# A one-core kernel of eight batches: its opening laid out anew

## Chip, cores and metric

The kernel runs on one core of a Trainium2 chip. The metric is the device time of one execution in microseconds (us), the median of the runs.

## What is computed

The input x has 8 batches of 512 rows of 256 values; ctx has 8 batches of 1601 rows of 256. Four layers follow each other, each added to x with a gain tanh(g), each on a layer norm of x:

```python
x = x + tanh(g_xattn[0]) * A(norm(x), ctx)   # one head: softmax(q Wq Wk' ctx' / 16 + mask) ctx Wv'
x = x + tanh(g_ffn[0])   * B(norm(x))        # self-attention, 4 of 16 heads of 64, picked per batch by a router
x = x + tanh(g_xattn[1]) * C(norm(x), ctx)   # 16 heads of 16 over ctx, integer mask shared by all batches
x = x + tanh(g_ffn[1])   * D(norm(x))        # mixture of 8 experts, each row to one, hidden size 1024
```

The router of B takes the mean of the normed x over the rows, times Wr, a softmax, and the 4 largest of 16. Everything is float32. In C the kernel splits q and k into three bfloat16 parts each, whose products give the scores.

## The kernel before, in words

Every engine has an instruction list of its own, written out in Python; semaphores tie them together. A batch of C is a loop of NU = 208 steps: 4 groups of 4 heads, 13 blocks of 128 ctx rows. Step u makes one transposed score of 99 x 128 x 512 in bfloat16 (`scores_t`, L1599), ACT takes its exponential (L1108), and every fourth step has the weighted sums of four heads (`values_c`, L1616). Ahead of the group that is being worked on, the scores of the next one are made once more, untransposed, in 64 pieces (`scores_c`, L1568), only for the row maxima, which DVE reduces (`maxima`, L2176); the table PIECES says how many pieces a step has. In and between these steps the layers A and B of the next batch (`prepare`) and the first part of A of the batch after it (`start_next`) are worked off; a Plan gives the step of each of their parts: XA, XB, XC the transposes of the normed x (`turn_x`, L1186) for A, B and C, QG the product with gA (`project_qg`, L1193), S the 16 scores of A (`score_a`, L1214), T the 16 transposes of their exponentials (`turn_a`, L1230), PV the 26 weighted sums of A (`weigh_a`, L1242), OA A's output product, K and V the projections of C (L1271, L1441), RL the router (L1281), QB, KB, VB, SB, TB, PVB, OB layer B (L1296, L1307, L1319, L1338, L1353, L1361, L1372), QC the query projection of C (L1389), LA, LB, LC the layer norms.

Before the loop there is the opening, W_END = 226 steps: batch 0 by the Plan FIRST, the beginning of batch 1 by SECOND, and from step 186 on the 64 first score pieces of batch 0 (W_PIECE), two a step. In each step every engine does `prepare(0, w, FIRST)`, then `start_next(0, w, FIRST)`, then `start_next(1, w, SECOND)`. The order in a list is the order of execution: an engine that waits holds up all that stands behind.

The layer norm goes from engine to engine: DVE makes statistics (L1897, L1903) and the variance (L1905), POOL the root (L819), DVE the normalisation (L1910), TensorE the transposes, ACT the copies out of PSUM (L967). PSUM has eight banks: MB (two), F0, F1, F2, SB (two), VB. In A of batch 0 the scores take turns in MB, F0, F1, the transposes in F2 and SB[0]; in A of batch 1 the scores take turns in F0 and F1 and all transposes are in F2. DVE adds the mask to a score and takes its maximum (`add_mask`, L1924); ACT makes the exponential (`exp_a`, L971), copies each transpose (`evac_pa`, L979, L982) and makes the high part of K (`high_k`, L989) into one of two buffers kp; DVE takes the rest (L1986), POOL splits it (L825, L827), SP stores the three parts (L592) to dramK. The query of C is kept in tq and qp, which lie in the place of ctxN; SP stores it with 6 DMAs per half (L614).

SP issues the weights, the stores, the loads of K, Q and V, and the gathered weights of B (L581, L585, after the router). POOL issues x, ctx, ctxT and the masks of A, in the order of its list. In the opening it also runs one `partition_all_reduce` (L911), whose result tells whether the mask of C hides anything. TensorE reads this flag ahead of step 186 and takes one of two copies of all that follows:

```python
            for w in range(W_PIECE[0]):
                open_step(w)
            pe.wait_ge(v_mf, 1)
            masked = pe.value_load(mflag[0:1, 0:1], min_val=0, max_val=1)
            pe.wait_ge(ld["ones"], 32)
            with pe.If(masked != 0):
                attend(True)
            with pe.Else():
                attend(False)
```

Of batch 1's 26 weighted sums of A, 7 stand in the opening (steps 216 to 224); the other 19 stand in steps 0 to 23 of the loop over batch 0, after which come A's output product (step 29) and the rest of batch 1.

## Time and profile before

| | |
|---|---|
| median of 3 runs | 2822.28 us (2820.21 to 2825.11) |
| the profiled execution | 2816.4 us, its span 2814.6 us |
| busy share of the span | TensorE 94%, DVE 61%, ACT 51%, POOL 10% |
| mean granted clock of TensorE | 0.989 of full |

The span is the time from the first to the last instruction. The opening takes the first 259 us of it, the loop over the batches follows, and the experts of layer D close it. TensorE's matmuls are pipelined: a group's busy time can be longer than the distance of its starts, and a float32 product is recorded as two passes.

### The profile page before, as it was taken

To read this page: it belongs to the slowest core of one execution; us is meant where nothing else is said; L and a number is where in the kernel's file an instruction comes from. 1 tells how busy PE (TensorE), PEld (TensorE's weight loads), DVE (VectorE), ACT (ScalarE), POOL (GpSimd) and SP (SyncE) were. 2 spreads that over 40 slices of the span, in tenths; PEclk is the share of its full clock that TensorE was granted. 3 is DMA by queue.
4 is the path that set the end of the run, shared out by engine and by line. 5 is a ranking of instruction groups with operands and counts; after the bars stand their busy time and mean duration, and the time that the engine had idled before them with its cause. 6 is when DMAs were issued, how large, how long until landed. Compare 5 with 4: busy or idle time off the path is not lost.

```text
span 2814.6 us, 39400 instructions
## 1 busy us (share of the span) xinstructions
PE 2632.1 (94%) x13626; PEld 1283.8 (46%) x13626; DVE 1729.8 (61%) x4198; ACT 1447.7 (51%) x2923; POOL 281.8 (10%) x344
## 2 busy tenths in 40 slices
PE   7878999999999999999999999999999989999998
PEld 3534433344334434443335433443444323349998
DVE  3346677577765776667666776677666768853111
ACT  2232565546554565456554656456545745663332
POOL 1200100011000200020001100020002000002221
PEclk9988999999999999999999999999999999999999
DMA  5431322423132413241232313241224023169995
GB/s 185 119 102 53 88 58 56 109 61 98 42 110 53 120 41 99 55 122 34 79 92 64 88 42 110 60 120 42 90 57 104 19 52 74 34 205 375 369 363 169
DMA packets 215140, 296.36 MB, mean 105 GB/s; under 512 B 50533, under 2 KB 180813, under 8 KB 214934
## 3 DMA queue, kind: packets, MB, share of 16 engines
q1 hardware_dynamic: 198428, 221.50, 28.1%
q0 software_dynamic: 16512, 72.32, 7.5%
q8 instruction: 110, 1.80, 0.3%
q14 instruction: 90, 0.74, 0.1%
HBM read 232.87 MB, written 60.50 MB: 104 GB/s over the span
## 4 chain that ended last, share of the span: by engine, by line
PE 78%; DVE 9%; ACT 6%; issue 5%; SPq 1%; DMA 1%; POOL 0%; ACTq 0%; POOLq 0%; DVEq 0%
PE PS L1616 12%; PE PS L1568 10%; PE PS L1599 10%; PE PS L1242 7%; DVE mxC L2176 6%; PE PS L1214 6%; PE PS L1751 5%; PE PS L1761 5%; PE PS L1271 3%; PE PS L1441 2%; PE PS L1338 2%; PE PS L1361 2%; ACT reg L1108 2%; PE PS L1230 2%; ACT reg L995 2%
## 5 line engine op out<-in xcount | busy, mean ns | idle before, releaser
L1108 ACT ACTIVATE reg<-PS 128x512 f32<-128x512 f32 (+1 forms) x1664 | 962.3, 598 | 946.2 <-PE PS L1599 940.0
L2176 DVE TENSOR_REDUCE mxC<-PS 128x1 f32<-128x400 f32 (+1 forms) x2048 | 1091.0, 570 | 529.4 <-PE PS L1568 513.6
L1568 PE MATMUL PS<-reg 96*128 96x400 bf16 (+1 forms) x2048 | 665.3, 339 | 51.6 <-DVE mxC L2176 20.8
L1599 PE MATMUL PS<-reg 99*128 99x512 bf16 (+1 forms) x1664 | 606.7, 384 | 23.0 <-ACT reg L1108 18.5
L1616 PE MATMUL PS<-reg 128*17 128x512 f32 (+1 forms) x3328 | 439.6, 600 | 1.1 <-DVE reg L2200 0.7
L1568 PEld LDWEIGHTS PS<-reg 96*128 96x128 bf16 x2048 | 195.2, 98 | 519.9 <-DVE mxC L2176 375.5
L1599 PEld LDWEIGHTS PS<-reg 99*128 99x128 bf16 (+1 forms) x1664 | 164.0, 100 | 351.0 <-ACT reg L1108 191.1
L1214 PE MATMUL PS<-reg 128*128 128x512 f32 (+1 forms) x512 | 209.8, 524 | 14.5 <-DVE small L1924 13.8
L1242 PE MATMUL PS<-reg 128*128 128x512 f32 (+1 forms) x416 | 211.5, 601 | 0.7 <-ACT reg L982 0.7
L1141 ACT ACTIVATE reg<-PS,reg 128x128 f32<-128x128 f32 x312 | 89.0, 368 | 197.9 <-PE PS L1751 110.4
L1751 PEld LDWEIGHTS PS<-reg 128*128 128x128 f32 x1248 | 145.0, 192 | 2.7 <-issue 0.9
L1751 PE MATMUL PS<-reg 128*128 128x128 f32 x1248 | 146.0, 275 | 0.0
L1761 PE MATMUL PS<-reg 128*128 128x256 f32 x624 | 141.6, 378 | 0.0
L1214 PEld LDWEIGHTS PS<-reg 128*128 128x128 f32 x512 | 88.8, 193 | 80.8 <-issue 51.1
L1761 PEld LDWEIGHTS PS<-reg 128*128 128x128 f32 x624 | 115.2, 189 | 15.0
L1616 PEld LDWEIGHTS PS<-reg 128*17 128x17 f32 (+1 forms) x3328 | 55.2, 95 | 145.3 <-issue 107.9
L819 POOL TENSOR_TENSOR rstd<-vpe,mhalf 128x4 f32<-128x4 f32 x32 | 33.1, 1034 | 857.6 <-DVE vpe L1905 847.9
L1924 DVE CUSTOM_DVE_ANT_0 reg<-PS,reg 128x512 f32<-128x512 f32 (+1 forms) x128 | 72.6, 570 | 72.1 <-PE PS L1214 69.4
L1271 PE MATMUL PS<-reg,wkC 128*128 128x400 f32 (+1 forms) x256 | 103.1, 513 | 6.0 <-DVE reg L1986 6.0
L1992 DVE TENSOR_REDUCE nmB<-PS 128x1 f32<-128x512 f32 x128 | 84.8, 682 | 26.3 <-PE PS L1338 26.3
L1441 PE MATMUL PS<-wvC,reg 128*128 128x256 f32 (+1 forms) x416 | 100.1, 379 | 0.0
L1242 PEld LDWEIGHTS PS<-reg 128*128 128x128 f32 (+1 forms) x416 | 76.1, 193 | 49.9 <-issue 40.0
(268 smaller groups left out, 2513.9 us busy)
## 6 DMA issues: line engine op xcount, KB each, us to landing
reg<-in_D_W SPq DMA_DIRECT2D x78, 1024.0 KB
reg<-in_A_mask POOLq DMA_DIRECT2D x32, 800.5 KB, 6.6
dramK<-reg SPq DMA_DIRECT2D x144, 100.0 KB
dramV<-reg SPq DMA_DIRECT2D x48, 272.0 KB, 3.1
reg<-in_ctxT POOLq DMA_DIRECT2D x8, 1601.0 KB, 9.7
reg<-in_ctx POOLq DMA_DIRECT2D x8, 1536.0 KB, 7.7
dramQ<-reg SPq DMA_DIRECT2D x96, 128.0 KB
reg<-dramQ SPq DMA_DIRECT2D x32, 384.0 KB, 5.8
```

The source lines that it names most:

```text
L1108: act.activation(pr[u % RING][0:r, :], PS[0:r, S_PLAN[NU * b + u][0], :], ACT.Exp).then_inc(a_expC, 1)
L1141: act.activation(hT[:, m, :], PS[:, bank, at:at + TS], ACT.Relu, bias=b1[par][:, m:m + 1]).then_inc(a_h, 1)
L1214: last = mm(PS[:, ring_a(n, i), 0:w], qgA[:, k, t * P:(t + 1) * P], ctxT[:, k, c0:c0 + w], start=k == 0, stop=k == KD - 1)
L1242: last = mm(PS[:, FB[m], :], ctxN[0:r, c, m * P:(m + 1) * P], ptA[0:r, c, :], start=c == 0, stop=c == CT - 1)
L1271: last = mm(PS[:, k_bank(n, u), 0:w], wkC[:, k, m * P:(m + 1) * P], ctxT[:, k, c0:c0 + w], start=k == 0, stop=k == KD - 1)
L1441: last = mm(PS[0:rows(c), v_bank(n, i), c % 2 * D:(c % 2 + 1) * D], ctxT[:, k, c * P:c * P + rows(c)], wvC[:, k, :], start=k == 0, stop=k ...
L1568: last = mm(PS[:, bank, 0:w], qs[(NG * bb + g) % 3][0:ROWS, h, t * P:(t + 1) * P], ks[g % 2][0:ROWS, h, c0:c0 + w], start=True, stop=True)
L1599: last = mm(PS[0:r, bank, :], ks[g % 2][0:STK, h, c * P:c * P + r], qs[(NG * b + g) % 3][0:STK, h, :], start=True, stop=not with_mask)
L1616: last = mm(PS[32 * h:32 * h + DC + 1, VB, :], vc[0:r, c, g * GH + h, :], pr[(UN * g + GH * c + h) % RING][0:r, :], start=c == 0, stop=c = ...
L1751: last = mm(PS[:, bank, at:at + TS], w1[j % WB][:, k, m * P:(m + 1) * P], xsT[j % 2][:, k, :], start=k == 0, stop=k == KD - 1)
L1761: last = mm(PS[:, VB, 0:D], hT[:, m, :], w2[j % WB][:, m, :], start=m == 0, stop=m == FM - 1)
L2176: v.tensor_reduce(mxC[:, h, t, j:j + 1], PS[:, M_PLAN[bb, g, i][0], 0:M_CH[j][1]], AX.X, ALU.max).then_inc(v_mx, 1)
```

## The change

- x of batch 0 is the first DMA of SP (it was one of POOL's), and DVE scales gA at step 7, behind the layer norm, and no longer first.
- Transposes of A take turns in three banks, in batch 0 (F2 and both SB) and in batch 1 (F2, VB, F0). Batch 1's scores have VB and SB[1] for the first two and then MB and SB. The two halves of the normed x of batch 0 are transposed into two banks, F2 and F1. ACT's exponential of a tile stands one step before that tile's first transpose.
- The K parts of batch 0 have eight buffers, in places of memory that are not yet in use; two K projections stand after the first four V projections. The sum for the router comes from ACT's copies (accum_out), not from a reduction on DVE.
- tq and qp of batch 0 lie elsewhere, so that ctxN of batch 1 loads from step 77, behind batch 0's weighted sums. Half of batch 0's Q stores are issued by ACT.
- Batch 1's masks each have a buffer: two are loaded by POOL at step 48, two by SP at step 147.
- qg and the first scores of batch 1 stand in layer B of batch 0 (steps 139 to 148); the branch stands ahead of step 152, in the layer norm of C, and no longer ahead of 186.
- The first score pieces of batch 0 go to steps 194 to 225. All 26 weighted sums of batch 1 stand in the opening: 18 in steps 206 to 224, four ahead of the transposes of the row maxima (step 231) and four behind. The opening has 237 steps.

The diff, cut:

```diff
-FIRST = Plan(SC=49, OA=(75, 77), LB=79, XB=(86, 88), RL=92, K=[78, 80, 94, 96, 98, 99, 100, 101],
-             V=[79, 81, 82, 90, 93, 95, 97], QB=(104, 105), KB=(106, 107), VB=(108, 109), LA=0, XA=(7, 9),
+FIRST = Plan(SC=49, OA=(75, 77), LB=79, XB=(86, 88), RL=92, K=[85, 87, 94, 96, 98, 99, 100, 101],
+             V=[78, 79, 81, 82, 90, 95, 97], QB=(104, 105), KB=(106, 107), VB=(108, 109), LA=0, XA=(7, 9),
              SB=O_SB, TB=[O_SB[i // 2] + 6 + 2 * (i % 2) for i in range(16)], PVB=(O_SB[3] + 11, O_SB[7] + 11),
              OB=(150, 151), LC=153, QG=(10, 12), XC=(161, 163), QC=(165, 167),
              S=[14, 15, 16, 17, 18, 19, 20, 21, 26, 27, 28, 29, 34, 35, 36, 37],
              T=[22, 23, 24, 25, 30, 31, 32, 33, 38, 39, 40, 41, 43, 44, 45, 46],
              PV=[48 + c for c in range(2 * CT)], wrap=0, ctx=0)
-SECOND = FIRST._replace(LA=100, XA=(112, 115), QG=(153, 155),
-                        S=[168, 170, 172, 174] + [178 + 10 * t + d for t in range(3) for d in (0, 2, 4, 6)],
-                        T=[178 + 10 * t + 2 * j for t in range(QT) for j in range(4)],
-                        PV=[216 + c for c in range(sum(u < NU for u in U_PV))], ctx=180)
+SECOND = FIRST._replace(LA=100, XA=(112, 115), QG=(139, 142),
+                        S=[145, 148, 164, 166] + [170 + 8 * t + d for t in range(3) for d in range(4)],
+                        T=[174 + 8 * t + d for t in range(3) for d in range(4)] + [198, 200, 202, 204],
+                        PV=[206 + c * 20 // 18 for c in range(18)] + [226, 227, 228, 229] + [232, 233, 234, 235], ctx=77)
 U_RAMP, U_MARK, U_RANK, U_SUM, U_TAB, U_SLOT = 2, 41, 46, (60, 75, 90, 112, 126, 140), (156, 157), (158, 159, 160, 161)
 U_TJ, U_ONE, U_IDS, U_WL = (162, 163, 164, 165, 166), (167, 168, 169, 170, 171, 172, 173), 190, (157, 158, 159)
-W_PIECE, W_ROWS = (186, 218), 222
-W_END = 226
+W_BRANCH, W_PIECE, W_ROWS = 152, (194, 226), 231
+W_END = 237
...
         return (MB + (F0, F1))[i % 4]
-    return (F0, F1)[i % 2] if n == 1 else F0
+    if n == 1:
+        return (VB, SB[1])[i] if i < 2 else (MB + SB)[(i - 2) % 4]
+    return F0
 
 
 def turn_a_bank(n, i):
 
     if n == 0:
-        return (F2, SB[0])[i % 2]
-    return F2 if n == 1 else F1
+        return ((F2,) + SB)[i % 3]
+    return (F2, VB, F0)[i % 3] if n == 1 else F1
+
+
+def qg_bank(n, k):
+
+    return (VB, SB[1])[k] if n == 1 else (F0, F1)[k]
+
+
+def x_bank(L, k):
+
+    return (F2, F1)[k] if L in (norm_a(0), norm_b(0), norm_c(0)) else F2
...
+                return eA0[t]
+            return eA0[(t + 2) % 4] if n == 1 else eA[t % 2]
...
+        kp0 = kp + [regC[:, w0:w0 + KPW].bitcast(BF16).rearrange("p (r c) -> p r c", r=3)
+                    for w0 in [k_at + KPW * i for i in range(5)] + [q_at]]
+        qg1 = regC[:, kr_at:kr_at + KD * S].rearrange("p (k q) -> p k q", k=KD)
...
+            sp.dma_start(xin, a["x"][0:1].rearrange("o (t p) n -> p (o t) n", p=P)).then_inc(ld["x0"], 16)
             sp.dma_start(qgA, a["A_WqWk"].rearrange(k2, p=P)).then_inc(ld["a"], 16)
...
-                    sp.wait_ge(kd_stored[i], 48 * (4 * n + 2 * (g // 2) + half + 1))
+                    sp.wait_ge(kd_stored[i], 48 * (4 * n + 2 * (g // 2) + half + 1 if n else 4))
...
+                    if n or r < NR // 2:
+                        sp.dma_start(dramQ[n, 8 * m:8 * m + 8, r * DC:(r + 1) * DC, :],
+                                     q_part(n, m, part)).then_inc(qd_stored[m], 16)
...
+                if w == SECOND.PVB[1] + 1:
+                    sp.wait_ge(pe_pvB, 2)
+                    for t in (2, 3):
+                        sp.dma_start(wA(1, t), a["A_mask"][1, t * P:(t + 1) * P, :]).then_inc(ld[f"mq{t}"], 16)
...
-            load_x(0)
             load_ctxT(0)
...
+                if m == 1 and u == 48:
+                    pool.wait_ge(pe_ptA, 16)
+                    load_mask(m, 0)
+                    load_mask(m, 1)
+                if m > 1 and u == p.PVB[1] + 1:
...
+                if m == 1 and u == p.ctx:
+                    pool.wait_ge(pe_otA, 2)
+                    load_ctx(m)
+                if m > 1 and u == p.ctx:
...
+            def evac_sum(L, k):
+                act.wait_ge(pe_xT, 2 * L + k + 1)
+                act.activation(xT[:, k, :], PS[:, x_bank(L, k), :], ACT.Copy,
+                               accum_out=msum[:, k:k + 1]).then_inc(a_xT, 1)
...
-                past(act, kd_stored[u % 2], 48 * (4 * n + u // 2))
-                act.activation(kp[u % 2][:, 0, 0:w], PS[:, k_bank(n, u), 0:w], ACT.Identity,
+                if n:
+                    act.wait_ge(kd_stored[u % 2], 48 * (4 * n + u // 2))
+                elif u == 2:
...
-                    if u + p.wrap == p.PV[CT * (k + 1) - 1] + 1:
-                        act.wait_ge(pe_otA, 2 * n + k + 1)
-                        act.activation(otA[:, k, :], PS[:, (F0, F1)[k], :], ACT.Copy).then_inc(a_otA, 1)
+                    if n != 1 and u + p.wrap == p.PV[CT * (k + 1) - 1] + 1:
+                        evac_ota(n, k)
...
-                    if u == p.S[4 * t + 3] + 2:
+                    if u == (p.T[4 * t] - 1 if m < 2 else p.S[4 * t + 3] + 2):
...
+                for m in range(KD):
+                    if w == FIRST.QC[m] + 6:
+                        act.wait_ge(v_qs, m + 1)
+                        for r in range(NR // 2, NR):
+                            act.dma_start(dramQ[0, 8 * m:8 * m + 8, r * DC:(r + 1) * DC, :],
+                                          q_part(0, m, QPART[r])).then_inc(qd_stored[m], 16)
...
-                elif n == 1:
-                    pe.wait_ge(v_ttr, 16 * n + i - 1)
-                elif n == 0:
-                    past(pe, v_ttr, i - 3)
-                if n == 1 and i < 2:
-                    pe.wait_ge(v_tq, i + 1)
-                elif n > 1 and i:
+                elif n == 0 and i >= 4 or i >= 5 and n == 1:
+                    pe.wait_ge(v_ttr, 16 * n + i - 3)
...
-                    past(pe, a_ptA, 16 * n + i if n else i - 1)
+                    past(pe, a_ptA, 16 * n + i - (2 if n < 2 else 0))
...
-                if p.wrap and u + p.wrap in p.PV:
+                if n > 1 and u + p.wrap in p.PV:
...
-                for w in range(W_PIECE[0], W_END):
+                for w in range(W_BRANCH, W_END):
...
-            for w in range(W_PIECE[0]):
+            for w in range(W_BRANCH):
...
-                if u == p.XB[1] + 2:
-                    dve.wait_ge(a_xT, 2 * norm_b(n) + 2)
-                    v.tensor_reduce(msum, xT, AX.X, ALU.add).then_inc(v_ms, 1)
...
-            dve.wait_ge(pe_set, KD)
-            v.tensor_scalar(gA[:], PS[:, 0:KD, 0:D], 1.0 / 16.0, None, ALU.mult).then_inc(v_set, 1)
+            def scale_g():
+                dve.wait_ge(pe_set, KD)
+                v.tensor_scalar(gA[:], PS[:, 0:KD, 0:D], 1.0 / 16.0, None, ALU.mult).then_inc(v_set, 1)
...
+                if w == 7:
+                    scale_g()
```

## Rows read from the trace of the kernel before

**Rows 1.** The page: busy time of the engines, and TensorE's slices.

```profile
PE 2632.1 (94%) x13626; PEld 1283.8 (46%) x13626; DVE 1729.8 (61%) x4198; ACT 1447.7 (51%) x2923; POOL 281.8 (10%) x344
...
PE   7878999999999999999999999999999989999998
```

**Rows 2.** Busy time of each engine in two stretches (start:end, length, engines, clock, DMA).

```profile
core 0: us, PE busy (x) PEld busy (x) DVE busy (x) ACT busy (x) POOL busy (x), PEclk, DMA share, GB/s
0.00:258.80 258.80, 205.24 (x716) 109.24 (x716) 118.00 (x296) 71.34 (x137) 32.46 (x49) 0.93 0.37 117
258.80:296.00 37.20, 36.33 (x141) 13.49 (x142) 20.00 (x39) 14.61 (x25) 0.00 (x0) 0.95 0.21 53
```

**Rows 3.** Timeline from 0 to 40 (start, length, engine, line; idle before and its cause).

```profile
9.17 1.39 DVE L1897 BATCH_NORM_STATS2 st<-reg 128x6 f32<-128x256 f32 x4
...
17.59 5.26 PE L1193 MATMUL PS<-reg,gA 128*128 128x512 f32 x8 [0.69 <-ACT reg L967]
...
23.54 11.41 PE L1214 MATMUL PS<-reg 128*128 128x512 f32 x32 [0.69 <-ACT reg L1009]
```

**Rows 4.** DMA issues from 0 to 60: KB each, us to landing.

```profile
reg<-in_A_WqWk SPq DMA_DIRECT2D x1, 512.0 KB, 3.9
reg<-in_x POOLq DMA_DIRECT2D x1, 512.0 KB, 7.2
```

**Rows 5.** TensorE's timeline from 34 to 63, batch 0's transposes.

```profile
34.79 1.04 PE L1230 MATMUL PS<-ident,reg 128*128 128x128 f32 x8
...
38.17 0.33 PE L1230 MATMUL PS<-ident,reg 128*65 128x128 f32 x1 [1.44 <-ACT reg L979]
...
47.43 7.41 PE L1214 MATMUL PS<-reg 128*128 128x512 f32 x16
...
62.58 22.63 PE L1242 MATMUL PS<-reg 128*128 128x512 f32 x52 [0.69 <-ACT reg L982]
```

**Rows 6.** Timelines of TensorE, ACT and SP around the K projections.

```profile
117.75 5.61 PE L1271 MATMUL PS<-reg,wkC 128*128 128x400 f32 x8 [6.01 <-DVE reg L1986]
...
116.34 0.59 ACT L989 ACTIVATE reg<-PS,bkC 128x400 bf16<-128x400 f32 x1 [6.87 <-DMA dramK<-reg]
...
108.78 2.53 SPq L585 DMA_DIRECT2D bs<-in_B_b  x4
```

**Rows 7.** TensorE's timeline from 165 to 187, around normalisation C.

```profile
165.07 3.72 PE L1372 MATMUL PS<-woB,reg 128*128 128x256 f32 x16 [0.85 <-DVE reg L2117]
...
178.04 1.09 PE L1186 MATMUL PS<-ident,reg 128*128 128x128 f32 x4 [5.81 <-issue]
...
186.66 6.07 PE L1214 MATMUL PS<-reg 128*128 128x512 f32 x16
```

**Rows 8.** Timelines of DVE and POOL there.

```profile
171.67 0.17 DVE L1905 TENSOR_SCALAR vpe<-mv 128x4 f32<-128x4 f32 x1
...
138.09 0.38 POOL L911 PARTITION_ALL_REDUCE small<-small  x1 [8.38 <-issue]
...
175.47 1.05 POOL L819 TENSOR_TENSOR rstd<-vpe,mhalf 128x4 f32<-128x4 f32 x1 [9.65 <-issue]
```

**Rows 9.** Timelines of TensorE and DVE, from 201 to 260.

```profile
205.88 1.49 PE L1568 MATMUL PS<-reg 96*128 96x400 bf16 x4 [4.69 <-issue]
...
258.82 0.39 PE L1599 MATMUL PS<-reg 99*128 99x512 bf16 x1 [2.94 <-DMA reg<-mrow]
...
215.58 0.69 DVE L1924 CUSTOM_DVE_ANT_0 reg<-PS,reg 128x512 f32<-128x512 f32 x1 [2.52 <-DMA reg<-in_A_mask]
...
244.45 7.85 DVE L2176 TENSOR_REDUCE mxC<-PS 128x1 f32<-128x400 f32 x16 [0.17 <-PE PS L1568]
```

**Rows 10.** Groups of instructions from 258.8 to 296 (count, busy us, mean ns, idle before).

```profile
L1242 PE MATMUL PS<-reg 128*128 128x512 f32 (+1 forms) x38 | 21.0, 634 | 0.0
L2176 DVE TENSOR_REDUCE mxC<-PS 128x1 f32<-128x400 f32 (+1 forms) x37 | 19.8, 570 | 21.1 <-PE PS L1568 21.1
```

**Rows 11.** Stretches of 5 us with a low clock (columns as in rows 2).

```profile
225.00:230.00 5.00, 5.00 (x14) 2.68 (x15) 2.47 (x6) 1.29 (x3) 0.00 (x0) 0.66 0.02 9
...
240.00:245.00 5.00, 4.73 (x18) 2.98 (x18) 4.42 (x10) 1.91 (x4) 0.00 (x0) 0.50 0.00 0
```

99 lines of the change are left out of this document (68 added, 31 removed).

## The prediction

> **What bounds the kernel now.** I read the page first: TensorE is busy for 94% of the span, and the slices show that it has room in two places only, the first four of the forty and two near the end [rows 1]. The change touches nothing near the end, so the question is what the opening costs. I cut it into two stretches [rows 2]: up to batch 0's first transposed score (258.8 us; TensorE is busy for 205.2, part of that at the lower of its two clock levels, 1.2 instead of 2.4 GHz), and the next 37.2 us, in which 19 weighted sums of batch 1 stand (busy 36.3). An instruction taken out of the loop is worth its full length if TensorE sets the pace there; put into a hole of the opening it costs nothing. Then I went along TensorE's timeline and asked at each hole which engine ended it [rows 3 to 9].
>
> **Start.** DVE begins x's statistics at 9.17, behind the scaling of gA, which waits for the setup products. x itself took 7.2 us from its issue on POOL, against 3.9 for A_WqWk, first on SP [rows 3, 4]. With x first on SP I let it land at 4.7, as A_WqWk did, and A_WqWk, now behind it and beside ctxT, at 7.0 to 8.0. The normalised x is there near 9.5, but the setup products (3.8 us) stand ahead of the transposes on TensorE and end at about 11.2. The transposes take 2.2, with a bank each and so without the copy between them, then copy 0.7, qg 3.4 to 5.3 (3.4 at 2.4 GHz; 5.26 before, half of it at 1.2 [rows 3]) and copy 0.7: first score at 18.2 instead of 23.54. **−5.3** (−3.5 to −6.5).
>
> **Batch 0's transposes.** One tile's four transposes are 1.6 us of work, but from 34.79 to the next score there are 3.6: ACT has the next tile's exponential between two copies, and TensorE waits up to 1.44 for a bank [rows 5]. With three banks, and the exponential issued behind the fourth copy, beside the next scores, the wait goes at two tiles: −3.9. The 16 products at 47.43 took 7.41 against half of 11.41 for 32 at 23.54 [rows 3, 5], since the clock fell behind such waits: −1.7. At the last two tiles the exponential follows the copies and is waited for in one piece: 6.9 instead of 7.9, from 54.67 to 62.58. **−6.5** (−3 to −8).
>
> **K and V projections.** TensorE waits 6.01 before 117.75 because ACT waited 6.87 for a store of K out of one of two kp buffers, and the next 8 products run cold, 5.61 instead of 2.8 [rows 6]. Eight buffers remove both, 8.8. A second bank for the transposes of x and ACT's sum in place of DVE's reduction remove 1.0 (a wait for a copy as the 0.69 before qg [rows 3], and a short one for the sum); the sum adds 0.2 to two copies, under a V projection of 1.7. Next late are the gathered weights: SP issues the four loads of biases behind those of the weights, until 111.3 [rows 6], and by my count the last lands 11.5 behind the routing product, whose end moves with TensorE, while K7 is through 10.8 behind it. That gives back 0.7 (0 to 3). If POOL's two operations per K fall behind, the range takes it in. **−9.1** (−6 to −10).
>
> **Batch 0's FFN attention.** It gains two qg products and two scores of batch 1, 4 × 1.74 = 6.9 of work on TensorE (a pass of 512 columns takes 22.63 / 52 = 0.435 [rows 5], each has four), among waits for copies and divisions of 0.5 to 0.85, of which the last is [rows 7], 3.1 together. **+3.9** (+3 to +6; ACT has two more copies in a full stretch).
>
> **Normalisation C.** From the end of the output projection (168.8) to the transposes at 178.04 are 9.25 us, though DVE has the variance at 171.84. POOL's root starts at 175.47 with "issue" as its cause, 9.65 after the mask DMAs; the same POOL lost 8.38 before its all-reduce at 138.09 [rows 7, 8]. I read this as POOL changing its program to the all-reduce and back, the way back starting only once the queue is past mask loads that wait for batch 0's second weighted sum. The change takes these loads away from here (two to step 48, two to SP); the way back starts behind the all-reduce and is over some 25 us before the root, which then follows the variance: 3.0 and the 2.6 from root to transposes, 5.6 instead of 9.25. **−3.6** (0 if the way back waits for the variance). The branch cost TensorE 4.69 where it stood [rows 9]; it lies in these 5.6 now, which hold no other work of TensorE, and is covered with 0.9 to spare. Without that cover it costs up to 4.69. The Q projections then take 9.4 from their first transpose, against 8.6 to 186.66 [rows 7]: two scores of batch 1 more (1.9), two waits for copies less. **+0.8** (−1 to +3, by how long the clock stays low).
>
> **From the Q projections to the first transposed score.** Before: 186.66 to 258.82, 72.2 us: the branch, products at half clock behind it, DVE held for batch 1's third mask until 215.58, so that the maxima run only from then on, and 2.94 for the copy of the row maxima [rows 9]. That mask's load stood behind POOL's wait for both Q stores. After: masks and ctxN are there. Twelve scores and transposes of batch 1, three times 5.6 + 1.6 [rows 3, 5], 21.8. Then 64 first scores in 32 steps: 12 steps by DVE (24 maxima × 0.49, from 16 in 7.85 [rows 9]), 11.8; 20 steps by TensorE (40 × 0.17 and 18 weighted sums × 0.87), 22.5. Four more sums 3.5, transposes 0.3, and four sums (3.5) that cover the 2.94. Sum 63.3. **−8.9** (−2 to −13). The six Q store issues on ACT stand before its copies while TensorE has scores for 5.6: nothing, and by SP's pace (0.6 each [rows 6]) 3.8 if uncovered.
>
> Opening: −5.3 − 6.5 − 9.1 + 3.9 − 3.6 + 0.8 − 8.9 = −28.7; first transposed score at 230.
>
> **Loop.** 38 passes × 0.435 = 16.5 leave its first 37.2 us [rows 10]. Its 37 maxima take 18 to 20 of DVE, the exponentials 14.6 of ACT [rows 2, 10], and TensorE keeps some 17 of work. Step by step, with the slowest of the three (ACT 2.4 for steps 0 to 3; DVE 4.0, 4.5, 4.5 for the next twelve; TensorE 2.7 and 2.7), it becomes 20.9: **−16.4** (−9 to −17). Later steps keep their work.
>
> Sum −45.1. The clock also fell to the low level at 225 and at 240, in the stretch that DVE paces [rows 11]; more such holes stand in the new one and in the loop's first steps: +3 (0 to 8). For waits that the trace of before can't show (code fetched behind a moved branch, DMA issues on ACT, banks shared by the two batches): +2 (0 to 6). −40.1: the profiled execution goes from 2816.4 (span 2814.6) to 2776; it stands 5.9 under the median of the runs, 2822.3, so I predict 2782.
>
> **Rivals.**
> (a) *The loop gives little back.* First and transposed scores wait for each other in turn through the two MB banks, DVE at 0.6 to 0.7 a maximum; the 24 steps take 29 and 8 is lost: 2790. Against: TensorE idles for only 0.9 of the 37.2 [rows 2].
> (b) *The next late thing in the opening.* POOL's way back still in the norm (3.6), weights late by 3, crowding in the attention (2): +8.6, 2791.
> (c) *Slower: TensorE's clock.* If waits short and often held it at 1.2 GHz from the Q projections to the loop's step 24, its work there (22 + 30 + 7 + 17) would double, less 11 that lie under DVE's pace: +65, 2847; the sign turns when the low level lasts for some 45 us of that work. For it: 0.50 at 240, 0.66 at 225 [rows 11]. Against: it was back within 5 us each time. The Trainium skill ("TensorE: Matmul & The Clock Gate", on oscillation) has a kernel with short pieces of work between waits fall to the low clock at every piece; by that rule this rival is the outcome, and the trace bears it out in part only.
> (d) *More*: no unseen waits and the clock high throughout: 2771.
>
> The Trainium skill ("Runtime: NRT & Kernel Launch", instruction fetch mechanics) says that a taken branch breaks the sequential fetch and stalls for a load of code; the 4.69 of the trace agree.
>
> **Numbers.** Forecast 0.54 (its own range 2774 to 2790), (a) 0.14, (b) 0.16, (c) 0.03, (d) 0.11, a gain under 0.2% 0.02. Two measurements of this kernel tell apart about 0.2%, 5.6 us. Range 2768 to 2800. Faster 0.95, same 0.02, slower 0.03.
>
> **What would show it.** In the profile after: first score near 18; no wait of 1.4 among the transposes of batch 0's first two tiles; K projections without a hole and at most a small one for the gathered weights before QB; POOL's root right behind the variance; an "issue" hole of about 5.6 before norm C's transposes and none before the first scores; no DVE wait for a mask; first transposed score near 230 and the loop's first 24 steps in some 21. It is wrong if those stay over 28, or if the first scores and sums (36 to 40 us) take over 48.

## The result and the profile of the changed kernel

| | before | after |
|---|---|---|
| median | 2821.24 us (4 runs, 2815.25 to 2825.11) | 2778.44 us (4 runs, 2776.35 to 2781.13) |
| the profiled execution | 2816.4 us, span 2814.6 | 2776.35 us, span 2774.5 |

The ratio is 0.9851, with an interval of 0.9831 to 0.987: 43 us less. 2782 was forecast. The two spans differ by 40.1 us, and a ledger of them can be made by the starts of the same instructions on TensorE in both traces. The last column is what the prediction had for the part.

| part, from and to which start on TensorE | before | after | difference | forecast |
|---|---|---|---|---|
| 0 to the first score of batch 0 | 23.5 | 16.8 | −6.7 | −5.3 |
| to its first weighted sum | 39.0 | 32.1 | −6.9 | −6.5 |
| weighted sums, to the first K or V projection | 26.9 | 26.9 | 0 | 0 |
| K and V projections, to the gathered product (QB) | 33.7 | 26.2 | −7.6 | −9.1 |
| batch 0's FFN attention, to its output projection | 41.9 | 46.3 | +4.4 | +3.9 |
| output projection and normalisation C, to its transposes | 13.0 | 11.0 | −2.0 | −3.6 |
| Q projections | 8.6 | 7.9 | −0.7 | +0.8 |
| to the first transposed score | 72.2 | 64.1 | −8.0 | −8.9 |
| loop, to batch 1's output product of A | 42.1 | 29.9 | −12.2 | −16.4 |
| the rest | 2513.7 | 2513.3 | −0.4 | 0 |
| clock and waits that could not be seen | | | in the rows above | +5 |

Each row rests on one execution of each kernel, and some rows are less sharp than they look. A second trace of the changed kernel has a span of 2774.2 us, but 27.6 us for the K and V projections (26.2 here) and 40.2 us from the first score piece to the first transposed score (41.8 here). The trace of the first experiment below, whose code is that of the kernel before in the first two parts, has 25.2 and 37.3 us there instead of 23.5 and 39.0: the sum is the same, the split between the two is not.

The page's busy row and slices, to be read beside [rows 1]: TensorE does the same 13626 instructions, and the first slices are fuller.

```profile
PE 2617.1 (94%) x13626; PEld 1276.9 (46%) x13626; DVE 1721.6 (62%) x4190; ACT 1447.8 (52%) x2939; POOL 280.3 (10%) x341
...
PE   8989999999999999999999999999999989999998
```

The two stretches of [rows 2], with the columns told there, cut at the first transposed score (231.3) and here at batch 1's output product (261.2):

```profile
0.00:231.30 231.30, 204.80 (x754) 110.67 (x755) 119.28 (x295) 69.96 (x140) 30.32 (x46) 0.98 0.43 132
231.30:261.20 29.90, 25.72 (x123) 6.15 (x122) 22.32 (x45) 17.16 (x31) 0.00 (x0) 1.00 0.30 73
```

The opening now holds 38 passes more (754 instead of 716) and is 27.5 us shorter. TensorE's busy time in it is the same, because the clock is 0.98 in place of 0.93. In the second stretch TensorE was busy for nearly the whole time before; now 4.2 of 29.9 us are holes.

The timelines answer to [rows 3], [rows 5] and [rows 9]. x's statistics begin at 4.84 instead of 9.17; qg's products take 3.71 and not 5.26; the transposes of the first tile (28.04) stand in one piece with the third tile's scores right behind; the first score piece of batch 0 (189.50) has no stall in front of it.

```profile
4.84 1.41 DVE L1976 BATCH_NORM_STATS2 st<-reg 128x6 f32<-128x256 f32 x4 [3.26 <-DMA reg<-in_x]
...
12.41 3.71 PE L1271 MATMUL PS<-reg,gA 128*128 128x512 f32 x8 [0.69 <-ACT reg L1018]
...
28.04 1.62 PE L1306 MATMUL PS<-ident,reg 128*128 128x128 f32 x13
29.50 5.71 PE L1288 MATMUL PS<-reg 128*128 128x512 f32 x16
...
189.50 0.85 PE L1647 MATMUL PS<-reg 96*128 96x400 bf16 x4
```

Around the K projections ([rows 6] before), TensorE, ACT and SP. The hole of 6.01 is gone, but one of 1.85 stands in its place. ACT waits 3.09 for a store of V, and SP issues that store at 93.19, behind six issues for K that took 3.83.

```profile
98.95 2.93 PE L1349 MATMUL PS<-reg,wkC 128*128 128x400 f32 x8 [1.85 <-DVE reg L2067]
...
97.28 0.38 ACT L1087 ACTIVATE reg<-PS 65x256 f32<-65x256 f32 x1 [3.09 <-DMA dramV<-reg]
...
89.32 3.83 SPq L632 DMA_DIRECT2D dramK<-reg  x6
93.19 0.46 SPq L661 DMA_DIRECT2D dramV<-reg  x1
...
98.06 2.53 SPq L625 DMA_DIRECT2D bs<-in_B_b  x4
```

Around normalisation C ([rows 7, 8] before): POOL's root starts at 155.04, right behind DVE's variance (154.77, which takes 0.17), where it came 3.6 us late before. But POOL's next operation, the residual with its bias (L886), runs from 156.08, and DVE's normalisation beside it takes 3.07 where it takes 1.38 without (8.25, in the start).

```profile
159.30 1.94 PE L1259 MATMUL PS<-ident,reg 128*128 128x128 f32 x8 [7.40 <-DVE reg L1989]
...
154.77 0.17 DVE L1984 TENSOR_SCALAR vpe<-mv 128x4 f32<-128x4 f32 x1
156.13 3.07 DVE L1989 TENSOR_SCALAR reg<-reg,mv,rstd 128x256 f32<-128x256 f32 x4 [1.19 <-POOL rstd L863]
...
8.25 1.38 DVE L1989 TENSOR_SCALAR reg<-reg,mv,rstd 128x256 f32<-128x256 f32 x4 [1.30 <-POOL rstd L863]
...
L1989 DVE TENSOR_SCALAR reg<-reg,mv,rstd x4: 404/404/2097, 156.1 to 158.8; 128x256 f32<-128x256 f32 x4
...
155.04 1.06 POOL L863 TENSOR_TENSOR rstd<-vpe,mhalf 128x4 f32<-128x4 f32 x1 [39.10 <-DVE vpe L1984]
156.08 2.00 POOL L886 TENSOR_TENSOR reg<-reg,boC 128x1024 f32<-128x1024 f32 x1
```

The line without a start gives the shortest, median and longest of DVE's four in ns: one took 2.10 us, the others 0.40 each, as in the start. In the kernel before, the same addition of POOL came 45 us behind the normalisation, since the loads of ctxN and of two masks, with their waits, stood ahead of it in POOL's list:

```profile
221.84 2.01 POOL L842 TENSOR_TENSOR reg<-reg,boC 128x1024 f32<-128x1024 f32 x1
```

The change took those loads away from there, and so brought the addition beside the normalisation.

Behind the Q projections, the Q stores that ACT now issues hold its exponential for 3.04, and TensorE waits 1.07 for it:

```profile
173.99 1.67 PE L1306 MATMUL PS<-ident,reg 128*128 128x128 f32 x13 [1.07 <-ACT reg L1027]
...
169.14 3.02 ACTq L1187 DMA_DIRECT2D dramQ<-reg  x3
172.21 1.63 ACT L1027 ACTIVATE reg<-reg,small 128x1601 f32<-128x1601 f32 x1 [3.04 <-issue]
```

In the loop's first steps DVE's maxima come in runs with holes of 0.68 between them, and each hole lies beside a set of weighted sums on TensorE (L1695, 1.05):

```profile
238.12 4.63 DVE L2256 TENSOR_REDUCE mxC<-PS 128x1 f32<-128x400 f32 x9 [0.68 <-PE PS L1647]
243.43 1.59 DVE L2256 TENSOR_REDUCE mxC<-PS 128x1 f32<-128x400 f32 x3 [0.69 <-PE PS L1647]
...
242.07 1.05 PE L1695 MATMUL PS<-reg 128*17 128x512 f32 x8
```

### The profile page after: what moved, and what is told of

Its sections match the earlier page's. It is cut to its first block, busy times and chain, and to the rows that moved or that the text cites. A ratio compares the mean times of both kernels' runs of the same rounds, so it can differ in the third digit from the quotient of the medians.

```text
span 2774.5 us, 39396 instructions
## 1 busy us (share of the span) xinstructions
PE 2617.1 (94%) x13626; PEld 1276.9 (46%) x13626; DVE 1721.6 (62%) x4190; ACT 1447.8 (52%) x2939; POOL 280.3 (10%) x341
## 4 chain that ended last, share of the span: by engine, by line
PE 78%; DVE 9%; ACT 6%; issue 4%; SPq 2%; DMA 1%; POOL 0%; ACTq 0%; POOLq 0%; DVEq 0%
PE PS L1695 12%; PE PS L1647 10%; PE PS L1678 10%; DVE mxC L2256 7%; PE PS L1320 7%; PE PS L1288 6%; PE PS L1830 5%; PE PS L1840 5%; PE PS L1518 2%; PE PS L1415 2%; PE PS L1349 2%; PE PS L1438 2%; ACT reg L1175 2%; PE PS L1306 2%; PE PS L1430 2%
## 5 line engine op out<-in xcount | busy, mean ns | idle before, releaser
L1695 PE MATMUL PS<-reg 128*17 128x512 f32 (+1 forms) x3328 | 439.5, 600 | 1.1 <-DVE reg L2280 0.7
L1288 PE MATMUL PS<-reg 128*128 128x512 f32 (+1 forms) x512 | 204.4, 515 | 14.3 <-DVE small L2005 13.4
L1320 PE MATMUL PS<-reg 128*128 128x512 f32 (+1 forms) x416 | 211.1, 600 | 0.8 <-ACT reg L1038 0.8
L1695 PEld LDWEIGHTS PS<-reg 128*17 128x17 f32 (+1 forms) x3328 | 55.2, 95 | 144.5 <-issue 107.7
```

The costliest lines, as they stand in the source:

```text
L1288: last = mm(PS[:, ring_a(n, i), 0:w], qg(n)[:, k, t * P:(t + 1) * P], ctxT[:, k, c0:c0 + w], start=k == 0, stop=k == KD - 1)
L1320: last = mm(PS[:, FB[m], :], ctxN[0:r, c, m * P:(m + 1) * P], ptA[0:r, c, :], start=c == 0, stop=c == CT - 1)
L1695: last = mm(PS[32 * h:32 * h + DC + 1, VB, :], vc[0:r, c, g * GH + h, :], pr[(UN * g + GH * c + h) % RING][0:r, :], start=c == 0, stop=c = ...
```

## The experiments

The spans of single executions can be told apart only so far. In the unchanged loop, the distance between the output products of A of two batches is 302.8 us for most pairs (300.3 to 300.9 for the first), but 0.3 to 2.9 more for one to three pairs of each trace, and the last 700 us (697.1 to 700.4) differ by up to 3.3 us between traces. So an edit is judged by its own part of the ledger, and by whole times only where several runs stand behind them. Even a part can differ between traces with the same code in it, by 2 us and more at the K and V projections; where that matters, the other traces are named.

### POOL's way back to its ordinary program

To the kernel before, one small addition on POOL right behind the all-reduce, so that the ordinary program is wanted there and not only at the root:

```diff
 pool.partition_all_reduce(..., bass.bass_isa.ReduceOp.max).then_inc(g_set, 1)
+pool.tensor_tensor(small[:, 40:44], mhalf[:], mhalf[:], ALU.add).then_inc(g_set, 1)
```

> The kernel before, with one tiny POOL addition (128x4) right behind the all-reduce, so that POOL meets an ordinary instruction there and not first in normalisation C. Theory (POOL changes its program to the all-reduce and back, and the way back starts only when an ordinary instruction comes up in the queue): the addition carries a hole of 8 to 10 us, and the root of normalisation C starts within 0.2 us of the variance instead of 3.6 behind it; the stretch from the end of the output projection to the transposes goes from 9.25 to 5.6 us, 3.6 less in the total. Rival (the two mask loads keep POOL busy writing descriptors for 9.6 us): the root stays 9.6 us behind the mask issues, the stretch stays 9.2.

Measured: 2815.87 us, 2819.69 for the kernel before beside it, one run each, within the spread of the kernel before (2815.25 to 2825.11). POOL's timeline (compare [rows 8]):

```profile
137.64 0.38 POOL L911 PARTITION_ALL_REDUCE small<-small  x1 [7.63 <-issue]
145.94 0.19 POOL L913 TENSOR_TENSOR small<-mhalf 128x4 f32<-128x4 f32 x1 [7.92 <-issue]
...
172.00 1.06 POOL L819 TENSOR_TENSOR rstd<-vpe,mhalf 128x4 f32<-128x4 f32 x1 [6.11 <-DVE vpe L1906]
```

The addition takes the 7.92 us upon itself, the root stands right behind the variance, and the transposes of C start at 174.58, 3.5 sooner. The loss behind the all-reduce is the cause of the late root, and not the mask loads, which stand where they stood. It comes with the next ordinary instruction, not when the all-reduce ends. In the changed kernel that instruction is the root itself, which waits 39.10 for the variance, and the loss is hidden in this wait. That it is a change of POOL's program is a reading of these rows; they show the loss, not what it is made of. The root is forward here too, and no addition of POOL meets the normalisation (it comes at 220.44): TensorE's transposes start 9.4 behind its output projection, against 11.0 in the changed kernel. The mask behind which DVE waited came 3.9 sooner as well (211.65 and 215.58), yet the first transposed score comes only 0.4 sooner. The windows say where the rest went: the same 127 passes from the mask to that score.

```profile
211.60:258.40 46.80, 38.80 (x127) 19.20 (x127) 33.84 (x81) 9.04 (x15) 2.55 (x2) 0.78 0.06 19
```

and in the kernel before:

```profile
215.50:258.80 43.30, 34.83 (x127) 17.58 (x127) 33.80 (x81) 9.03 (x15) 2.54 (x2) 0.88 0.07 21
```

TensorE's granted clock was 0.78 here and 0.88 there, and its passes took 4.0 us longer in sum, which is as much as the 3.5 that went missing.

The start of this trace says one thing more. Its code there is that of the kernel before, with the same holes among the transposes, yet the fourth tile's 16 products, which took 7.41 there [rows 5], are these:

```profile
49.11 5.71 PE L1215 MATMUL PS<-reg 128*128 128x512 f32 x16
```

In their place qg's products took 6.77 and not 5.26. The fall of the clock that the kernel before had at these products belongs to that execution, not to its holes.

### The residual copy held back

To the changed kernel:

```diff
 pool.wait_ge(v_oB, QT * (b + 1))
+if b == 0:
+    pool.wait_ge(v_xn, 4 * norm_c(0) + 4)
```

> The kernel after, with POOL's addition of the bias to the residual of batch 0 (128x1024, 2.0 us) held until DVE has normalised for layer C. In the kernel after it starts 1 us ahead of that normalisation's end and DVE's four instructions take 3.07 us instead of 1.38. Theory (the two engines slow each other when they read and write the same memory at once): the four take 1.4, the hole before TensorE's transposes goes from 7.4 to 5.7. Rival (DVE is slow there for another reason, such as the code that is loaded for TensorE's branch at the same time): they stay near 3.1.

Measured: 2775.82 us. DVE's normalisation and POOL's copy:

```profile
154.93 1.38 DVE L1991 TENSOR_SCALAR reg<-reg,mv,rstd 128x256 f32<-128x256 f32 x4 [1.19 <-POOL rstd L863]
...
156.83 2.00 POOL L888 TENSOR_TENSOR reg<-reg,boC 128x1024 f32<-128x1024 f32 x1 [1.94 <-DVE reg L1991]
...
156.41 1.94 PE L1261 MATMUL PS<-ident,reg 128*128 128x128 f32 x8 [5.71 <-DVE reg L1991]
```

The normalisation is back at 1.38, and TensorE's hole is 5.71 instead of 7.40, which is the 5.6 that the prediction had. So the collision alone cost the 1.7. The first transposed score came 2.4 sooner, and the loop to batch 1's output product took 31.9 instead of 29.9 in this execution (a clock of 0.71 and 0.61 from 230 to 240).

### A third bank in the loop's first steps

To the changed kernel: F2, free by then, as a third bank for the maxima of batch 0's first 40 steps, beside the two MB, with the two waits of TensorE that the bank then needs.

```diff
-window = spare_at(u)
+window = 3 if b == 0 and u < 40 else spare_at(u)
```

> The kernel after, with F2 as a third bank for the untransposed scores of batch 0's first 40 steps. In the kernel after, DVE idles 0.7 us behind each set of four weighted sums (1.0 us of TensorE), nine maxima take 5.3 instead of 4.5 us, and the first 24 steps take 25 us instead of the 20.9 forecast. Theory (two banks are too few to carry DVE over the sums): the idle goes at most sets, the first 24 steps take 21 to 22.5 and the first product behind them (A's output, at 261.2) starts 3 us sooner. Rival (DVE's own pace of 0.5 to 0.57 per maximum is the bound): 24 to 25, nothing moves.

Measured: 2773.75 us. DVE:

```profile
236.90 4.42 DVE L2260 TENSOR_REDUCE mxC<-PS 128x1 f32<-128x400 f32 x9 [0.25 <-PE PS L1651]
```

The hole in each run falls from 0.68 to 0.25, a maximum from 0.51 to 0.49, and the part from 29.9 to 26.7: −3.2. Of the 4.2 us that the loop gave back too little, the two banks hold at least three quarters.

### SyncE's order at the K and V projections

Two edits of one line, alone and in the changed kernel: the stores of batch 0's first two K pieces behind step 96 (behind V's store and the gathered weights), or behind step 92 (behind V's store only).

```diff
-if u == p.K[i] + 3:
+if u == (96 if n == 0 and i < 2 else p.K[i] + 3):
```

> The kernel after, with SP's stores of the first two K pieces put behind the loads of the gathered weights. In the kernel after, TensorE has a hole of 1.85 us before the last two K projections: ACT's copies of K stand behind its copy of V, which waits for a V store that SP issued late, behind six K store issues (3.8 us). The gathered weights come late by the same 3.8. Theory (both come from SP's order): the hole closes, layer B's first projection starts 1.5 to 2.0 us sooner. Rival (the hole is the store's own landing time, 4 us among other transfers): hole and start stay within 0.5.

Measured: 2776.71 us. The last K product set stands without a hole and the weights are issued from 92.21 on (94.95 in the changed kernel); V/K to QB takes 23.8 instead of 26.2. The 26.2 is one trace. In six others with the changed kernel's code there, the part takes 24.9, 25.2, 25.2, 25.6, 25.8 and 27.6, with a hole of 1.37 to 1.95 ahead of the last K products each time; with the stores moved it takes 23.8 here and 23.9 in the last experiment's kernel of four edits. Against these seven traces the edit is worth 1.1 to 3.8 us, mostly between 1 and 2.4.

> The changed kernel with the stores of the first two K pieces of batch 0 put behind step 92 of SyncE's order, so that the store of the fourth piece of V is issued ahead of them and not behind their six issues. All K stores but these keep their places. The theory (TensorE's hole of 1.85 us in the K and V part comes by way of ScalarE's V copy, which waits for a V store that SyncE issues late) expects that hole gone and the part to last about 24 us from the first K or V product to the router's gathered product, as where the two stores went to step 96 (23.8 instead of 26.2), and the ends of the batch 0 part 2 us sooner. The rival (the gathered weights, issued last, are what the part waits for) expects a hole of about 1 to 2 us just ahead of the gathered product, since the six issues now stand between V's store and the weights again. Span 2771 to 2775, since spells of low clock further on differ by up to 3 us between executions.

Measured: 2776.71 us. With step 92, TensorE and SP:

```profile
93.66 5.89 PE L1349 MATMUL PS<-reg,wkC 128*128 128x400 f32 x16
101.59 0.70 PE L1373 MATMUL PS<-reg 128*128 128x512 f32 x1 [2.04 <-DMA bs<-in_B_b]
...
89.19 3.83 SPq L632 DMA_DIRECT2D dramK<-reg  x6
94.58 2.91 SPq L621 DMA_DIRECT2D reg<-in_B_w  x4
97.67 2.53 SPq L625 DMA_DIRECT2D bs<-in_B_b  x4
```

V's store went ahead, all 16 K products run in one piece, and the 1.85 are gone. But now the gathered weights end TensorE's wait, 2.04: the part takes 25.8, the rival's reading. Both waits come from the same six issues on SP. Only with them behind both the store and the weights is the time saved. They are not enough by themselves, though: in the trace of the two transposing banks below, SP's order is the changed kernel's, V's store is issued 15.7 us behind the part's first product instead of 17.4 and lands 3.4 behind that instead of 4.1 (ACT waits 1.29 for it and not 3.09), all 16 K products run in one piece, and the part takes 24.1. What makes the store earlier there stays open. The gain of the first of the two edits did not reach the end in its only execution: 3.6 us ahead at the first transposed score (1.6 of it in score pieces that the edit does not touch), 2.2 at batch 1's output product (clock 0.82 and 0.84 from 240 to 250), nothing at the end.

### All Q stores on SyncE

```diff
-if n or r < NR // 2:
+if True:
     sp.dma_start(dramQ[...], ...)
```

and ACT's six issues left out.

> The kernel after, with all twelve Q stores of batch 0 issued by SP again. In the kernel after ACT spends 3.0 and 2.1 us on its six issues, its first exponential of batch 1 starts behind them, and TensorE waits 1.07 us for it before batch 1's first transpose. Theory (the issues cost ACT's queue and nothing waits for Q that early: its load lands 9 us before the first scores): that wait falls to 0.3 or less, from the Q projections to the first scores it takes 1.0 us less. Rival (SP's 12 issues, some 7.5 us, bring Q too late): the first scores wait 1 us or more.

Measured: 2776.38 us. In the trace the exponential follows its forerunner at once, and TensorE's transposes have no hole (171.30, 1.62, no wait); from the transposes of C to the first score piece are 29.1 us instead of 30.2. The 1.07 us was the price of the issues on ACT. The prediction had put it at nothing if covered and 3.8 if not. Again the gain is not in the whole time, though batch 1's output product came 3.1 sooner (only the 1.1 by this edit). The last 700 us lost it, in code that is the same. Two windows of 25 us there, of this kernel,

```profile
2299.20:2324.20 25.00, 22.48 (x123) 8.10 (x124) 15.59 (x39) 14.32 (x28) 0.00 (x0) 0.93 0.33 81
2324.20:2349.20 25.00, 23.04 (x121) 8.97 (x121) 18.87 (x58) 12.55 (x24) 3.03 (x2) 0.86 0.27 67
```

and of the changed one:

```profile
2299.00:2324.00 25.00, 22.18 (x132) 8.25 (x134) 16.80 (x42) 15.81 (x31) 0.00 (x0) 1.00 0.33 81
2324.00:2349.00 25.00, 22.91 (x139) 9.44 (x143) 21.90 (x65) 13.87 (x27) 3.02 (x2) 1.00 0.27 67
```

### The branch back behind the layer norm

```diff
-W_BRANCH, W_PIECE, W_ROWS = 152,
+W_BRANCH, W_PIECE, W_ROWS = 194,
```

> The kernel after, with TensorE's branch ahead of step 194 (the first scores) as in the kernel before, and no longer in normalisation C. Theory (the branch is wholly hidden by the normalisation): the stretch from layer B's output product to the transposes stays at 11.0 us, an issue hole of 4.7 us stands before the first scores, products behind it run at the low clock under DVE's pace, and the first transposed score comes 5 us later. Rival (the branch and the code behind it lengthen the normalisation in the kernel after): that stretch gets shorter by 1 us or more, and the cost of the move is 4 or less.

Measured: 2781.05 us. TensorE:

```profile
158.15 1.94 PE L1259 MATMUL PS<-ident,reg 128*128 128x128 f32 x8 [7.41 <-issue]
...
193.88 2.47 PE L1647 MATMUL PS<-reg 96*128 96x400 bf16 x7 [4.27 <-issue]
```

Out in the open the branch costs 4.27 us ahead of the first score pieces (4.69 in the kernel before), and the part from the transposes of C to them is 35.7 instead of 30.2. The first transposed score comes 3.0 later, not the 5 expected; from those transposes to it are 76.2 us instead of 72.0. In the norm the hole is 7.41 without the branch and 7.40 with it, and 5.71 with it where the copy is held back: there it is hidden wholly. (The profile calls the hole "issue" in one and "DVE" in the other. The name does not matter, the length does.)

### 19 of the weighted sums back in the loop

The changed kernel with the last 19 of batch 1's 26 weighted sums back in steps 0 to 23 of the loop; all else as changed.

```diff
-PV=[206 + c * 20 // 18 for c in range(18)] + [226, 227, 228, 229] + [232, 233, 234, 235], ctx=77)
+PV=[206 + c * 20 // 18 for c in range(7)], ctx=77)
```

> The kernel after, with batch 1's last 19 weighted sums of layer A back in the loop's first 24 steps; 7 stay in steps 206 to 212. Theory (in the opening the sums stand half under DVE's maxima and under the copy of the row maxima, in the loop they are paid nearly in full): the first transposed score comes 3.5 us sooner (at 228), the loop from there to batch 1's output product takes 42 instead of 30 us, and the total is 8 to 9 us longer. Rival (TensorE's work is worth the same in both places): the opening is shorter by 10 or more and the total is the same within 3.

Measured: 2784.71 us (4 runs, 2783.7 to 2786.41), ratio to before 0.9873 (0.9857 to 0.989). So the move of the 19 sums is worth 8.3 us of span (2782.8 and 2774.5); by the medians it is 6.3 us, and 8.7 against the changed kernel's later five runs. Some 32 of the 40 us between the spans are the rest of the change. From the first transposed score to batch 1's output product the loop takes 43.1, as long as before the change; the move gives 13.2 there, and the opening pays 4.7 for it between the first score piece and the first transposed score (37.2 and 41.8; 3.1 against the 40.2 of the changed kernel's second trace). That is little for 38 passes (16.5 us), because without them the stretch has holes and a low clock:

```profile
204.00:209.00 5.00, 4.84 (x18) 2.07 (x16) 4.40 (x9) 0.00 (x0) 0.00 (x0) 1.00 0.01 3
209.00:214.00 5.00, 4.20 (x11) 1.00 (x10) 5.00 (x12) 0.00 (x0) 0.00 (x0) 0.74 0.00 0
214.00:219.00 5.00, 5.00 (x12) 1.11 (x11) 5.00 (x12) 0.00 (x0) 0.00 (x0) 0.50 0.00 0
219.00:224.00 5.00, 2.01 (x7) 0.55 (x7) 3.69 (x11) 0.46 (x1) 0.00 (x0) 0.50 0.00 0
```

Where only score pieces are left for TensorE (from 208.8), it waits for DVE in turns, and its clock falls to the low level and stays there for the rest of the stretch. In the changed kernel the same stretch has sums between the pieces, and the clock stays high but for one window of 0.69.

### Two K buffers again

```diff
-return kp0[u] if n == 0 else kp[u % 2]
+return kp[u % 2]
```

with ACT's wait for the store of the buffer, as before the change.

> The kernel after, with two buffers for the K parts of batch 0 instead of eight; ACT's copies wait for the stores again. Theory (the eight buffers bring 8.8 us by themselves, less the 1.85 of the hole that the kernel after still has before the last K projections): layer B's first projection starts 7 to 9 us later, a hole of some 6 us behind DVE's rest of K, products at the low clock behind it. Rival (the new order of V ahead of K gives the stores enough time by itself): 3 us or less.

Measured: 2785.61 us. TensorE and ACT:

```profile
105.89 4.98 PE L1347 MATMUL PS<-reg,wkC 128*128 128x400 f32 x8 [7.59 <-DVE reg L2065]
...
104.49 0.59 ACT L1046 ACTIVATE reg<-PS,bkC 128x400 bf16<-128x400 f32 x1 [8.08 <-DMA dramK<-reg]
```

The part takes 35.2 instead of 26.2 us: +9.0 (+7.6 to +10.3 against the six other traces named above), and the span is 9.3 longer. Without the eight buffers nothing is gained in this part: it takes 1.5 more than before the change (33.7).

### Batch 0's transposes in two banks, the exponential at its old place

```diff
-return ((F2,) + SB)[i % 3]
+return (F2, SB[0])[i % 2]
```

and the exponential two steps behind a tile's last score.

> The changed kernel with batch 0's transposes of the weights back in two banks, and their exponential back at its old place, two steps behind the last score of a set instead of right ahead of the first transpose. The theory of the prediction (the third bank and the place of the exponential take away the holes that TensorE had in each set of 13 transposes) expects the holes of 0.25 and 1.44 us back in each of the four sets: from the first score of batch 0 to its first weighted sum 38 to 39 us instead of 32.1, the weighted sums of batch 0 later by as much (at about 55.3), and the span 5.5 to 7 us longer, 2780 to 2782. The rival (the earlier score alone made the gain, and the banks are a change of form) expects the 32.1 us to stay and the span of 2774 to 2776.

Measured: 2782.79 us. TensorE, with the holes of [rows 5]:

```profile
27.49 1.04 PE L1306 MATMUL PS<-ident,reg 128*128 128x128 f32 x8
28.78 0.66 PE L1306 MATMUL PS<-ident,reg 128*128 128x128 f32 x4 [0.25 <-ACT reg L1035]
30.88 0.32 PE L1306 MATMUL PS<-ident,reg 128*65 128x128 f32 x1 [1.44 <-ACT reg L1035]
...
40.13 5.71 PE L1288 MATMUL PS<-reg 128*128 128x512 f32 x16
```

From the first score to the first weighted sum are 37.3 us instead of 32.1: +5.2, of the 6.9 that the part gained. The other 1.7 is the clock: the fourth tile's 16 products (40.13) take 5.71 here, in spite of the holes, and took 7.41 before the change. So these holes do not bring that fall of the clock, and neither did the old start: the first experiment has both, and 5.71 too. The two executions of that code differ. It was a wrong attribution in the prediction, and luck that the sum is right. The 38 to 39 us for the part are missed by 0.7. The span, 2781.0, is where the expectation had it, but in part by luck: at batch 1's output product this trace is 3.4 us behind the changed kernel's, which is less than the 5.2, among other things since the K and V part is 2.1 shorter and the start 0.6; the rest of the 6.5 comes in code further on that is the same.

### Four edits together, beside the changed kernel

> The changed kernel with four edits tried one by one before: the residual copy on GpSimd held until the normalisation is over (1.7 us there), a third bank for the maxima in the first 40 steps of the loop's first batch (3.2 us there), the first two K stores of batch 0 behind step 96 (2.4 us there), and all of batch 0's Q stores issued by SyncE (1.1 us there). If the four add up, the opening and the first batch end 8 us sooner, and the time is about 2770 us (2768 to 2774, since part of a gain has been lost again to spells of low clock). The rival (they hit the same wait, or the spells eat them all) expects 2774 to 2778, no better than the changed kernel beside it on the same chip.

> The changed kernel itself, unaltered, for comparison with the kernel of four edits on the same chip and in the same rounds. Both theories expect 2776 to 2781 us, 41 to 43 us below the kernel before, as where it was first timed; the spread of its executions shows how much the spells of low clock take by themselves.

Measured, on one chip: the changed kernel again 2776.06 us (5 runs, 2774.47 to 2778.4), ratio 0.9846 (0.9833 to 0.9858); with the four edits 2767.19 us (5 runs, 2766.52 to 2770.78), ratio 0.9816 (0.9803 to 0.9828). The slowest run of the one lies below the fastest of the other, and 8.9 us lie between the medians. In the trace V/K to QB takes 23.9, the hole in the norm is 5.72, the transposes of C to the first score piece take 29.2, and the loop's part 26.7, so that each of the four parts has what its edit gave alone (2.2, 1.7, 1.0 and 3.2; 1.6 more lie between the first score piece and the first transposed score, a stretch that took 40.2 in the changed kernel's second trace too and 41.8 in its first, whose clock was low from 199.7 to 203.1). Gains that single executions had lost to spells of low clock are there in the median of five.

## Why the prediction held, and where its steps failed

**The sum.** Forecast were 40.1 us between the profiled executions, and their spans lie 40.1 apart. This is closer than its steps were. The opening without its clock and unseen terms was forecast at −28.7 and gave −27.5; the loop at −16.4 and gave −12.2; the two shortfalls, 5.4 together, are the size of the +5 put aside for clock and unseen waits. The clock had a part of some 1.6 in them, a low stretch that the changed kernel's second trace does not have there. From the first score piece to the first transposed score, code that is the same in ten traces takes 41.8 or 41.9 us in the five that have such a stretch and 40.2 in the five that have none:

```profile
199.70:203.10 3.40, 3.40 (x6) 1.51 (x7) 2.64 (x6) 0.00 (x0) 0.00 (x0) 0.50 0.00 0
```

The rest are the two engines' waits for each other in the loop and the collision in normalisation C, less terms that came out better than forecast. That these balance to a tenth of a us is luck. 2782 against 2778.44 is 3.6 too high for one reason: I added the 5.9 by which the profiled execution of before stood under its median, and the profiled one of after stands 2.1 under its own. Rival (d) was set down without that step: its 2771 is the profiled 2816.4 less 45.1, and as a median it would have been 2777, nearer to the measured 2778.44 than the forecast.

**Start** (−5.3, measured −6.7). A_WqWk landed at 6.23, not at 7 to 8, and the clock was high by qg (3.71), as forecast. Right mechanism, the term slightly too small; against the first experiment's start (25.2) it would be −8.4.

**Transposes** (−6.5, −6.9). The sum held. 5.2 are the bank and the exponential, taken back together, so that nothing tells how much each brings. The 1.7 "since the clock fell behind such waits" is a step that failed: the same waits stand in two other traces without that fall.

**K and V** (−9.1, −7.6). The eight buffers are worth 9.0. The step that failed is "next late are the gathered weights ... gives back 0.7". I counted SP's issues for the weights, but not the six K stores that more buffers let loose at once ahead of V's store and of the weights: 3.83 us of SP. Moving them behind both gives 2.2 to 2.4 against the profiled trace, 1.1 to 3.8 against the other six with this hole, and 0.2 to 0.3 against the one trace that has no hole in spite of them; so they are the cause of the hole together with the time that V's store takes, which no run separates. The range of the term (0 to 3) held what the profiled trace had.

**FFN attention** (+3.9, +4.4). The four groups of work and a few more short waits; no experiment was made on it.

**Normalisation C** (−3.6, −2.0). The late root is shown to come from the first ordinary instruction behind the all-reduce, by the addition put there. What failed is "the 2.6 from root to transposes", taken over from the profile of before. There POOL's next operation, the residual copy, ran too late to meet the normalisation (221.84), behind loads and their waits. The earlier root alone does not bring them together, as the first experiment shows. The change took those loads out of POOL's list, the two came together, and DVE took 1.7 longer. The branch is covered, as said: the hole is as long with it as without.

**Q projections and scores** (+0.8 and −8.9, measured −0.7 and −8.0). The masks and the branch no longer hold anything. The issues on ACT cost 1.07, between the two prices named for them (nothing and 3.8). The score pieces and sums took 34.4 from their start, as added up.

**Loop** (−16.4, −12.2). This is the largest miss of a term, and the mechanism of rival (a) at about half its price. I had taken the slowest engine for each step, as if the others never waited for it in turn. With two banks the pieces stop while TensorE does a set of weighted sums, DVE starves for 0.68, and the time isn't made good. The third bank gives 3.2 back, which shows it. SP's order and the collision are rival (b), some 3 to 4 us together and not 8.6.

**Clock** (+3; rival (c)). Rival (c) is not borne out: 0.98 over the opening, where it was 0.93. What the clock took ahead of the loop's first step is the 1.6 above and a low stretch in normalisation C, within the 0 to 8. The prediction's "back within 5 us each time" was read from windows of 5 us; in the trace of before the clock was 0.50 from 174.5 to 184.5, in normalisation C. By the Trainium skill ("TensorE: Matmul & The Clock Gate", on oscillation) short pieces of work between waits fall to the low clock at each piece. In the Trainium skill's kernel the waits are for DMAs, and longer than most here. The trace of the changed kernel doesn't agree; that with 19 sums back in the loop does in part, with 0.50 from 214 to 229 where TensorE had score pieces alone and then next to nothing.

## What to carry to other kernels

When a wait goes, look at what the waiting engine's neighbours do at the new time, and not only at what is late next: here more buffers let a batch of stores into a queue ahead of two things that were wanted sooner, and loads taken out of POOL's list brought its next addition beside DVE's normalisation. Where work is shared step by step between two engines through two buffers, a sum of the slower engine's times is a lower bound; add a hole for each burst of other work that is longer than the buffers can bridge. Judge an edit of a few us in a kernel of thousands by the distance between fixed instructions around it, look at how far that distance differs between traces whose code there is the same, and take several executions for the whole.

## What the runs showed of the hardware

- POOL lost 7.6 to 8.6 us ahead of the `partition_all_reduce` and 7.9 to 9.7 ahead of the next ordinary instruction (7.63 and 7.92 with the addition, 8.38 and 9.65 in the kernel before). In the changed kernel 8.63 stand ahead of the all-reduce, and the second loss does not show: the next ordinary instruction, the root, waits 39.10 for DVE anyway. A cheap instruction right behind moves the second loss to where nobody waits.
- A DVE normalisation out of and into SBUF (1.38 us for four) took 3.07 beside a POOL addition of 2.00 that had started 0.05 sooner: 2.10 for the first of the four, which ended 0.15 behind the addition, and 0.40 for each of the others. The Trainium skill ("SBUF — State Buffer", Who interferes with whom) says that a `tensor_scalar` of DVE in a two-port mode and a GpSimd operation exclude each other, the later one waiting for the whole of the first. By that rule it would be 1.95 of waiting and 1.38 of work, 3.33; the trace agrees within 0.3 us, though no view shows the mode itself, and I had not applied it.
- Three DMA issues on ACT took 3.02 us, 1.0 each, and the next three 2.05, 0.7 each, where SP's six K stores took 3.83, 0.64 each; ACT's next instruction waited behind the first three.
- TensorE's clock differs between executions of the same program: the changed kernel's first trace has 0.50 from 199.7 to 203.1, its second 1.00 there and 0.69 from 100 to 105. Between traces with the same code in a part, the last 700 us differ by up to 3.3 us and the loop's first 30 by up to 2. A gain ahead of such a place can vanish in one trace and be there in the median.
